# A graph attention sum pass, eight tiles a step: the one-hots read back from memory, the weighted features in three bf16 parts

## The reference

```python
h = (x_flat @ W_gat).reshape(M, HEADS, NUM_EXPERTS)          # 4 heads, 4 experts
e = leaky_relu(a_src[src] + a_dst[dst], negative_slope=0.2)  # a number per edge and head
e_max = segment_max(e, dst, num_segments=M)
ee = exp(e - e_max[dst])
denom = segment_sum(ee, dst, num_segments=M)
alpha = ee / (denom[dst] + 1e-16)
agg = segment_sum(h[src] * alpha[:, :, None], dst, num_segments=M)
```

## Time and profile before

| | |
|---|---|
| median of three runs | 15629.44 us |
| profiled execution, its own time | 15631.75 us |
| its span | 15630.1 us |
| busiest engine over the span | DVE 8606.0 us, 55% |
| max pass: first to last gather issued | 8265.4 to 9716.2 us |
| sum pass: first one-hot to last addition | 9746.51 to 10531.05 us |

### The profile page before, as it was taken

One profiled execution on the slowest core, in us unless ns is written; L12 is line 12 of the kernel. 1 busy time (PEld: TensorE's weight loads), 2 busy tenths in 40 slices (PEclk: granted clock), 3 DMA queues, 4 the chain that ended last, 5 costly groups with the idle time before them and its releaser, 6 DMA issues. The chain is left out here.

```text
span 15630.1 us, 202267 instructions
## 1 busy us (share of the span) xinstructions
PE 7593.7 (49%) x36846; PEld 5267.8 (34%) x36847; DVE 8606.0 (55%) x21695; ACT 2856.5 (18%) x7869; POOL 7784.0 (50%) x7181
## 2 busy tenths in 40 slices
PE   0000016666667625635555666995542249554274
PEld 0000002444444314513333333884411125333164
DVE  8977622777777731124446777771245557724413
ACT  0000011111122221110011111442111125321121
POOL 0287854777778645557756776002317740033211
PEclk9999997888888857877766666557765569767587
DMA  3000011666643304513321111004436665343143
GB/s 126 13 3 16 3 29 56 197 197 197 197 121 111 103 11 140 161 49 99 99 67 14 9 9 7 0 0 150 144 95 201 201 162 155 111 130 118 22 160 115
DMA packets 1154962, 1484.18 MB, mean 95 GB/s; under 512 B 334557, under 2 KB 923706, under 8 KB 1153533
## 3 DMA queue, kind: packets, MB, share of 16 engines
q1 hardware_dynamic: 838220, 879.49, 17.8%
q0 software_dynamic: 316464, 602.12, 14.7%
HBM read 1075.82 MB, written 405.67 MB: 95 GB/s over the span
## 5 line engine op out<-in xcount | busy, mean ns | idle before, releaser
L1297 DVE TENSOR_TENSOR l_acc<-l_acc,l_sum_o 128x260 f32 (+2 forms) x2496 | 1052.8, 422 | 792.0 <-PE l_sum_o L1211 606.6
L1211 PE MATMUL l_sum_o<-l_sum_rows,l_sum_s 128*128 128x256 f32 (+1 forms) x3328 | 1134.9, 483 | 519.4 <-DMA l_sum_rows<-l_feats,l_sum_ix 491.8
L815 POOL DMA_INDIRECT gat_max_rows<-gat_table,gat_max_ix x1080 | 1123.1, 1040 | 328.8 <-issue 307.2
L1513 POOL IOTA m_route_run_i<- 1x56 int32 (+2 forms) x4 | 0.6, 158 | 2099.2 <-SPq L1510 2099.2
L1211 PEld LDWEIGHTS l_sum_o<-l_sum_rows,l_sum_s 128*128 128x128 f32 x3328 | 680.5, 229 | 902.3 <-issue 540.8
L815 POOL DMA_INDIRECT l_max_rows<-pairs,l_max_ix x832 | 856.5, 1029 | 253.6 <-issue 238.7
L815 POOL DMA_INDIRECT l_sum_rows<-l_feats,l_sum_ix x832 | 844.6, 1015 | 264.4 <-issue 220.7
L815 POOL DMA_INDIRECT l_max_rows<-l_feats,l_max_ix x832 | 842.8, 1013 | 267.6 <-issue 226.4
L204 POOL DMA_INDIRECT gat_records<-l_sum_moved x624 | 809.4, 1297 | 236.6 <-issue 178.3
L949 PE MATMUL l_max_qe<-l_acc,l_max_st 128*128 x1664 | 592.3, 518 | 602.4 <-DVE l_max_prod L1000 601.5
L972 PE MATMUL gat_max_mx<-ident_b,gat_max_far 128*128 128x512 bf16 x1080 | 575.7, 533 | 520.9 <-DVE gat_max_top L1050 517.8
(11 more groups left out here) (668 smaller groups left out, 20647.4 us busy)
## 6 DMA issues: line engine op xcount, KB each, us to landing
along<-l_max_rows SPq DMA_DIRECT2D x208, 512.0 KB, 3.8
l_sum_rows<-along SPq DMA_DIRECT2D x208, 512.0 KB, 3.8
l_along<-l_max_rows SPq DMA_DIRECT2D x208, 512.0 KB, 3.4
l_sum_rows<-l_along SPq DMA_DIRECT2D x208, 512.0 KB, 3.5
m_ffn_w1b<-in_L_ffn_W SPq DMA_DIRECT2D x108, 512.0 KB, 4.3
m_ffn_w2b<-in_L_ffn_W SPq DMA_DIRECT2D x108, 512.0 KB, 5.1
m_ffn_xs<-sorted_rows SPq DMA_DIRECT2D x196, 256.0 KB, 3.8
m_results<-m_ffn_ys POOLq DMA_DIRECT2D x196, 256.0 KB
```

The costliest lines, as they stand in the source:

```text
L815: pool.indirect_dma_start(rows[:, j, :], None, table, bass.IndirectOffsetOnAxis(ap=ix[:, j:j + 1], axis=0), bounds_check=bound, oob_is_err ...
L1211: ins = pe.matmul(o[:, j, 0:R], s4[:, slot % G4 if H else slot, j, :], rhs, start=True, stop=True)
L1297: dve.tensor_tensor(a, a, o[:, j, 0:R].unsqueeze(1), ALU.add).then_inc(acc_own, 1)
```

## The change

gat_sum gets a function of its own, `gat_sum`, which handles eight tiles a step (135 steps' worth) instead of four. The one-hots are no longer built again: in the max pass SP stores each quad's one-hots (128 KB) to DRAM (`keep_s`), and DVE waits before it overwrites a slot until the store of eight quads before has landed. In the sum pass SP loads eight tiles a step (256 KB) into one of eight slots. The weighted numbers, 20 an edge, are split into three bf16 parts (high by ACT, remainder by DVE, middle by ACT, low by DVE), and PE multiplies a tile's bf16 one-hots by all 60 columns in one pass. DVE sums the three parts of eight tiles in one reduction from PSUM, then adds tile by tile. The cast of the one-hots to fp32 is gone. Lags, in order: PE collect 5, maxima 2, turn_s 1; ACT copy_st 1, expo 3, high 4, middle 4; DVE (largest first) add 6, weigh 4, exponent 2. The loop turns every eight steps. `edge_sum` loses its `kept` argument, which only this pass used; its other callers issue what they did.

```diff
--- edge_max
+        s_stored = [ph.sem(f"s_stored{k}") for k in range(S8)] if s_out is not None else None
+                def keep_s(q, slot):
+                    sp.wait_ge(s_ready, q + 1)
+                    sp.dma_start(s_out[:, ds(q * Q, Q), :], s4[:, slot]).then_inc(s_stored[slot], 16)
+                if s_out is not None:
+                    assert not stages
+                    steps(sp, n, [(0, keep_s)], unroll=S8, lead=16)
+                    for k in range(S8):
+                        sp.wait_ge(s_stored[k], 16 * len(range(k, n, S8)))
...
+                    if s_out is not None:                      # in onehot, ahead of L992
+                        wait_free(dve, s_stored[slot], (q - slot) * (16 // S8), q, S8)
--- gat_sum (new; H, W = 4, 16; R = 20, HA = 8, B = 8; n = L.tiles // B)
+            def _(sp):
+                def load(q, slot):
+                    wait_free(sp, out_done, q - 7, q)
+                    sp.dma_start(s8[:, slot], s_in[:, ds(q * B, B), :]).then_inc(s_loaded[slot], 16)
+                steps(sp, n, [(0, load)], unroll=S8, lead=8)
...
+                def turn_s(q, slot):
+                    pe.wait_ge(s_loaded[slot], (q - slot) * (16 // S8) + 16)
+                    wait_free(pe, st_ready, q - 1, q)
+                    for j in range(B):
+                        ins = pe.transpose(stp[:, slot % 2, j, :], s8[:, slot, j, :], core.ident_b[:])
+                    ins.then_inc(st_turned, 1)
+                def maxima(q, slot):
+                    b = blocks_of(nc, mybir.EngineType.PE, L, q, B)
+                    pe.wait_ge(st_ready, q + 1)
+                    wait_free(pe, e_own, (q - 1) * 4, q)
+                    for j in range(B):
+                        ins = pe.matmul(mep[:, slot % 2, j * 3 * HA:(j + 1) * 3 * HA], st[:, slot % 2, j, :],
+                                        ma_parts[:, ds(b[j], 1)].rearrange("p o k h -> p (o k h)"), ...)
+                    ins.then_inc(me_done, 1)
+                def collect(q, slot):
+                    pe.wait_ge(parts_own, (q + 1) * 2)
+                    wait_free(pe, part_ready, q - 1, q)
+                    for j in range(B):
+                        ins = pe.matmul(o[:, slot % 2, j * 3 * R:(j + 1) * 3 * R], s8[:, slot, j, :],
+                                        w3[:, slot % 2, j].rearrange("p k r -> p (k r)"), start=True, stop=True)
+                    ins.then_inc(out_done, 1)
+                steps(pe, n, [(5, collect), (2, maxima), (1, turn_s)], unroll=S8, lead=8, in_order=True)
...
+                def copy_st(q, slot):
+                    act.wait_ge(st_turned, q + 1)
+                    wait_free(act, me_done, q - 1, q)
+                    act.copy(st[:, slot % 2], stp[:, slot % 2]).then_inc(st_ready, 1)
+                def expo(q, slot):
+                    act.wait_ge(e_own, (q + 1) * 4)
+                    wait_free(act, parts_own, (q - 1) * 2, q)
+                    act.activation(wr[:, slot % 2, :, W:R], e[:, slot % 2], ACT.Exp).then_inc(ex_ready, 1)
+                def high(q, slot):
+                    act.wait_ge(wr_ready, q + 1)
+                    wait_free(act, out_done, q - 1, q)
+                    act.copy(w3[:, slot % 2, :, 0, :], wr[:, slot % 2]).then_inc(hi_ready, 1)
+                def middle(q, slot):
+                    act.wait_ge(parts_own, q * 2 + 1)
+                    act.copy(w3[:, slot % 2, :, 1, :], rest[:, slot % 2]).then_inc(mid_ready, 1)
+                steps(act, n, [(1, copy_st), (3, expo), (4, high), (4, middle)], unroll=S8, lead=8, in_order=True)
...
+                def weigh(q, slot):                            # exponent: as L1256 to L1275, on eight tiles
+                    dve.wait_ge(ex_ready, q + 1)
+                    r, x, w = wr[:, slot % 2], rest[:, slot % 2], w3[:, slot % 2]
+                    dve.tensor_tensor(by_head(r[:, :, 0:W]), by_head(kept[:, ds(q * B, B), H:]),
+                                      bc(r[:, :, W:R], 3, [P, B, H, W // H]), ALU.mult).then_inc(wr_ready, 1)
+                    yield                                      # three times
+                    dve.wait_ge(hi_ready, q + 1)
+                    ow.at(q)
+                    ow.mark(dve.tensor_tensor(x, r, w[:, :, 0, :], ALU.subtract))
+                    yield                                      # three times
+                    dve.wait_ge(mid_ready, q + 1)
+                    ow.mark(dve.tensor_tensor(w[:, :, 2, :], x, w[:, :, 1, :], ALU.subtract))
+                def add(q, slot):
+                    b = blocks_of(nc, mybir.EngineType.DVE, L, q, B)
+                    dve.wait_ge(out_done, q + 1)
+                    dve.tensor_reduce(part[:, slot % 2], o[:, slot % 2, 0:B * 3 * R]
+                                      .rearrange("p (q k r) -> p q r k", q=B, k=3), AX.X, ALU.add
+                                      ).then_inc(part_ready, 1)
+                    yield
+                    dve.wait_ge(part_ready, q + 1)
+                    for j in range(B):
+                        wait_free(dve, acc_own, q * B + j, q)
+                        a = acc[:, ds(b[j], 1), :]
+                        dve.tensor_tensor(a, a, part[:, slot % 2, j, :].unsqueeze(1), ALU.add).then_inc(acc_own, 1)
+                        yield
+                steps(dve, n, [(2, exponent), (4, weigh), (6, add)], unroll=S8, lead=8)
```

More of the change, by code:

```diff
@@ L816, in gather_quad, with blocks_of @@
                                 bounds_check=bound, oob_is_err=False).then_inc(sem, 16)
-def blocks_of(nc, engine, L, q):
-    _, vals = nc.values_load_multi_w_load_instructions(L.block[0:1, ds(q * Q, Q)], engines=(engine,),
+def blocks_of(nc, engine, L, q, tiles=Q):
+    _, vals = nc.values_load_multi_w_load_instructions(L.block[0:1, ds(q * tiles, tiles)], engines=(engine,),
                                                        min_val=0, max_val=T - 1,
@@ L827, in edge_max @@
 def edge_max(nc, core, L, name, heads, table, width, val, best, queries=None, extra=None, kept=None,
-             beside=None, along=None):
+             beside=None, along=None, s_out=None):
     H, W, dot = heads, width, queries is not None
@@ L1061, in _, with edge_sum @@
                       unroll=S8)
-def edge_sum(nc, core, L, name, acc, width, table=None, kept=None, heads=0, val=None, ma=None, slope=None,
+def edge_sum(nc, core, L, name, acc, width, table=None, heads=0, val=None, ma=None, slope=None,
              scale=1.0, along=None, beside=None, fold=False):
@@ L1077, in edge_sum @@
         assert not fold or (H == 1 and along is not None)
-        rows = ph.sb("rows", [P, G4, Q, R if fold else W]) if kept is None else None
+        rows = ph.sb("rows", [P, G4, Q, R if fold else W])
         s4 = ph.sb("s4", [P, G4 if H else S8, Q, P])
@@ L1121, in _ @@
                         mover.fetched_all(sp)
-            if kept is None and along is None:
+            if along is None:
                 @block.gpsimd
@@ L1172, in weigh_s @@
                     ins.then_inc(wide_ready, 1)
-                stages = [(0, index)] * (kept is None and along is None)
+                stages = [(0, index)] * (along is None)
                 if H:
@@ L1279, in weigh @@
                     dve.wait_ge(ex_ready, q + 1)
[L1280 to L1284, removed]
+                    dve.wait_ge(got[slot % G4], (q - slot % G4) * (per_quad // G4) + per_quad)
+                    src = rows[:, slot % G4]
                     r = wr[:, slot % 2]
@@ L2025, in layer1_ffn @@
     table = nc.dram_tensor("gat_table", [T * P, 4 + HE], F32).ap()
+    onehots = nc.dram_tensor("gat_onehots", [P, gat.tiles, P], BF16).ap()
     with ExitStack() as ctx:
```

71 lines of the change are left out of this document (69 added, 2 removed).

## The result

The changed kernel takes 15714.99 us, the median of four runs (15709.97 to 15719.57). The kernel before took 15628.29 us beside it (15613.09 to 15631.8, four runs). The ratio is 1.0057, with an interval of 1.004 to 1.0075: 87 us slower. The profiled execution took 15711.29 us for a span of 15709.6.

What follows compares the result with a forecast made beforehand. The sum pass was taken as bound by PE before and by a ring of waits after: 131 steps at 6.7 us plus 39 for fill and drain, 917 for 784.5, plus 132, giving 15762 us; range 15560 to 15890.

Steps and rivals of the forecast that it cites:

- the ring: Sum pass: closed chain of waits through PE, ACT and DVE, passed once per step, terms adding to 6.74 us.
- Collects: PE in the sum pass: eight bf16 products of 60 columns, put at 1.0 us from the maxima's 0.127 spacing.
- Register loads: PE's eight block numbers ahead of the maxima, partly hidden by collects: 0.2 us, bounds none to 1.0.
- DVE alone: DVE's own work per step of the sum pass, put at 5.1 us, so it would wait some 1.6 us.
- The loop's turn: Stall at each turn of the sum pass's loop, 15 times instead of 32: none added, 0.2 us a step at most.
- fill and drain: Start and end of the sum pass: 15 us fill and 24 us drain, 39 together.
- The max pass: Storing 128 KB of one-hots a quad there costs nothing, as POOL's gathers bind it; bounds minus 10 to plus 40 us.
- 1 (DVE the limit): Sum pass: handovers cost less, DVE's additions decide at 5.1 us a step; 15552 us, chance 0.15.
- 2: Sum pass: TensorE runs at 2.4 GHz, halving PE's 3.2 us of the ring; 15552 us, chance 0.06.
- 3: PE in the sum pass: collects 0.157 us a tile, register loads 0.8 bare, ring 7.55; 15873 us, chance 0.15.
- 4: Max pass: POOL's gathers queue behind the one-hot stores, plus 40 us on top; 15800 us, chance 0.05.

Runs made afterwards that it cites:

- E1: Changed kernel with PE's stages in the order maxima, turn_s, collect instead of collect, maxima, turn_s: 15509.75 us, ratio 0.9925 to the kernel before.
- E5: Changed kernel with PE loading the block numbers ahead of collect's wait instead of behind the collects: ratio 0.9988 to the kernel before, on another chip.
- E2: Changed kernel with all PE maxima reading block 0, so PE loads no block numbers and other blocks' attention maxima are left out: 15545.05 us.
- E11: Changed kernel with PE's order maxima, turn_s, collect and DVE's block-number loads behind the reduction, eight steps a turn: ratio 0.9895 to the kernel before.
- E4: Changed kernel with DVE's loop turning every four steps instead of eight: 15687.82 us.
- E6: Changed kernel with four tiles a step instead of eight: ratio 1.014 to the kernel before, on another chip.
- E12: Changed kernel with PE's collect last, DVE's block-number loads behind the reduction, and DVE's loop turning every four steps: 15423.77 us.

## Why the prediction was right, step by step

The direction, the mechanism and the range held; the loss was 87 us and not 132. All the ring's handovers are in the trace in the order in which they were written down, and E1, the same instructions in another order, shows that the ring made the change slow. Term by term, from the steady step:

| term | predicted | measured | where |
|---|---|---|---|
| low parts to first load | 0.12 | 0.05 | 10112.79 to 10112.84 |
| eight collects | 1.0 | 0.35 | E5, 10902.40 to 10902.75 |
| register loads on PE | 0.2 | 0.71 | 1.06 less the collects |
| eight maxima | 1.2 | 0.99 | 10113.90 to 10114.89 |
| transposes till the copy | 1.02 | 1.08 | to 10115.97 |
| copy, expo, till high starts | 1.12 | 1.04 | to 10117.01 |
| high, handover | 0.34 | 0.35 | to 10117.36 |
| remainder to end of low parts | 1.74 | 1.40 | to 10118.76 |
| ring | 6.74 | 5.97 | |

- **Collects: the most mis-sized term**, 1.0 for 0.35. I took the maxima's spacing of 0.127 as what a short bf16 product costs. E2 shows that 0.09 of it goes with the operand's register address: with a fixed one the maxima take 0.034 a tile (0.27 for eight). The collects, with 60 columns and a fixed address, stand (0.58 - 0.23)/7 = 0.05 apart, which is 60 columns at 1.2 GHz, the level that the granted 0.50 means.
- **Register loads** were put at 0.2 within bounds of none to 1.0, and 0.71 of them stands bare behind the collects. The 0.65 too much for the collects and the 0.51 too little here nearly cancel, which is luck and not insight.
- **DVE.** The additions stand 0.32 apart (10117.70 with 0.82 for three of 0.18), not 0.39. They now add from SBUF, before from PSUM, where each also waited for its own product. The Trainium skill (Perfetto Trace Analysis, Optimizing Scalar/DVE Operations) gives DVE's overhead as some 60 ns on SBUF and 125 on PSUM. The difference fits the trace's 0.07, but the page means busy time, and an addition's own record is 0.17 before and 0.18 now; no run here changes the memory alone. DVE alone needs 4.30 (E1), not 5.1.
- **The loop's turn** was put at nothing, because engines in a ring wait anyway. The trace shows 3.7 to 4.0 us of idle time at it. The next step, 4.30, gives some of it back, and yet 15 turns cost 44 us (50.7 for 8 × 5.97 = 47.8, 2.9 each, of which 0.37 is a gap between two additions in another step of the eight). Before, the same column had 0.51.
- **The sum.** 132, less 131 × 0.73 = 96 for the shorter ring, plus 44 for the turns, is 80, and the pass has 71; the rest is in fill and drain, put at 39, where the last two steps, for one, are 3.7 long and not 4.3 to 5.1. Errors of opposite sign made the total look better than its terms.
- **The max pass** was put at nothing within bounds of -10 to +40. By the traces above the stores cost it some 11 us on the mean: within the bounds, not nothing, and hidden in the pair of the result. The loads of 256 KB cost nothing: PE's transposes (L2012) follow the maxima without a gap. The longer stretch behind the pass, 11 us, was not foreseen.
- **Rivals.** 1 (DVE the limit) did not come, though E1 shows what it would have been: 4.30 a step. 2: the clock is 0.50 with PE at 42%, as it was at 96. The "activity" of which the Trainium skill speaks (TensorE: Matmul & The Clock Gate, Part 1, What's actually happening) was not tested by this change, since PE does less. 3: the collects are the opposite of dear; a load and a product in turn would be 0.157 apart and are 0.05. E2's eight weight loads of 128 columns for the maxima take 0.34 in all, under 0.05 each. So a load is hidden by the product although all rows of the array are used, and takes far less than 107 ns: the trace disagrees with the Trainium skill (TensorE: Matmul & The Clock Gate, LDWEIGHTS and The mechanism) as the prediction cites it. The rival's other half, dear register loads, held (0.71 for its 0.8). 4: not at +40, see the max pass.

## What to carry to other kernels

Before halving an engine's work, write down what its program order makes it wait for: an instruction that waits longest belongs last in the step, and here that one line was worth some 200 us. Work that needs no wait (register loads, addresses) belongs ahead of the wait on the engine whose wait is long, and behind a long instruction on the engine that is the limit. Price an edit after the order is right: the same read-back was worth nothing with the wrong one and 107 us with the right one. And look at several runs before a cost is called nothing: one pair of traces had the max pass at 1450.8 us with and without the stores, the others didn't.

## What the runs showed of the hardware

- Eight weight loads with bf16 products of 60 columns: 0.05 us a tile at the granted 0.50; of 24 columns 0.034 (E2); the latter with its moving operand addressed through a register 0.12.
- Eight block numbers into registers: 0.71 us bare on PE, 0.57 on DVE, none of it in a busy column; the record puts DVE's down to PE. Ahead of a long wait (E5) or behind a long instruction (E11) most of it is hidden.
- The stall at a loop's turn goes with the size of the body, and not in proportion: 0.51 before, 3.7 to 4.0 with eight steps in gat_sum, 0.48 over the usual with four (E4), and 0.48 over it with eight steps of half the tiles (E6).
- Dependent additions on DVE: 0.32 us apart from SBUF, 0.39 with one operand in PSUM (and one more semaphore to wait for).
- The granted clock in the sum pass is 0.50 with PE 96% busy (before), 42% (after), 55% (E1) and 65% (E12).
